# The order of small works at the pair boundaries of an attention kernel: three tables of unit numbers changed

## The reference

```python
x = x + _layernorm(_L0_attn_ref(_layernorm(x), wq, wk, wv, wo, q_norm_w, k_norm_w))
x = x + _layernorm(_L0_ffn_ref(_layernorm(x), gate_w, up_w, down_w, gate_s, up_s, down_s))
# attention: 32 query heads, 8 key/value heads of 64, RMS norm over the whole q and the whole k
xq = _rms_norm(x @ wq.T, q_norm_w, EPS)
xk = _rms_norm(x @ wk.T, k_norm_w, EPS)
xv = x @ wv.T
bias = where((dist <= 0) & (dist >= -256), slopes * dist, -inf)
attn = softmax(xq @ xk.T * scale + bias)
out = (attn @ xv) @ wo.T
# feed forward: ternary weights (-1, 0, 1) with a scale for each row
out = (silu((x @ gate_w.T) * gate_s) * ((x @ up_w.T) * up_s)) @ down_w.T * down_s
```

## Time and profile before

| | |
|---|---|
| median of 3 runs | 1192.66 us (1192.19 to 1193.7) |
| the profiled execution | 1192.59 us, span 1190.7 us |
| granted TensorE clock, mean | 0.998 |
| projection of four sequences | to about 291 us of the span |
| attention, pairs 0 to 3 (no output projection) | 291.1 to 414.6 us |
| attention, pairs 4 to 15 | 414.6 to about 882 us |
| rest | last output tiles, feed forward |

### The profile page before, as it was taken

The page is one execution under the profiler, slowest core; times in us unless marked ns, Lnnn a source line. Parts: engine busy times, 40 slices in busy tenths (PEclk is TensorE's granted clock), DMA queues, the critical chain, the costliest instruction groups (busy, mean ns, idle before and its releaser), DMA issues.

```text
span 1190.7 us, 26658 instructions
## 1 busy us (share of the span) xinstructions
PE 1161.0 (98%) x9016; PEld 991.1 (83%) x9016; DVE 888.5 (75%) x2329; ACT 743.6 (62%) x1583; POOL 304.6 (26%) x353
## 2 busy tenths in 40 slices
PE   7999999999999999999999999999999999999997
PEld 5878888887877798889988988898988888888876
DVE  5587778687899888888888888888866575645464
ACT  4645555455899888878888888888853443222230
POOL 3000000000788842423242333323211100202022
PEclk9999999999999999999999999999999999999999
DMA  5216355346676766556755575556445540303020
GB/s 177 106 45 247 143 201 223 124 195 255 209 237 232 246 208 201 170 190 197 220 159 187 182 226 163 154 171 209 138 134 186 168 141 2 107 1 107 1 71 37
DMA packets 100898, 189.55 MB, mean 159 GB/s; under 512 B 9376, under 2 KB 39072, under 8 KB 100768
## 3 DMA queue, kind: packets, MB, share of 16 engines
q1 hardware_dynamic: 100768, 187.88, 47.1%
HBM read 116.22 MB, written 71.63 MB: 158 GB/s over the span
## 4 chain that ended last, share of the span: by engine, by line
PE 92%; DVE 3%; ACT 2%; issue 1%; DMA 0%; POOL 0%; SPq 0%; POOLq 0%; DVEq 0%; ACTq 0%
PE bank L1408 21%; PE bank L1541 19%; PE bank L1473 15%; PE bank L1346 12%; PE bank L1434 12%; PE bank L1452 3%; PE bank L1450 3%; PE bank L1451 3%; PE bank L1462 2%; PE bank L1518 1%; PE bank L1373 1%; DVE pT_lo L1172 0%; ACT y_raw L937 0%; PE bank L1363 0%; ACT o_raw L925 0%
## 5 line engine op out<-in xcount | busy, mean ns | idle before, releaser
L802 ACT ACTIVATE p_sb<-u_sb,low 128x384 f32<-128x384 f32 (+2 forms) x512 | 271.7, 535 | 54.0 <-DVE low L1054 47.0
L1054 DVE CUSTOM_DVE_ANT_0 u_sb<-bank,bias 128x384 f32<-128x384 f32 (+2 forms) x512 | 229.1, 451 | 44.5 <-PE bank L1346 25.4
L1346 PE MATMUL bank<-k_st,q_st 128*128 128x384 f32 (+2 forms) x1024 | 252.3, 329 | 1.8 <-DVE low L1054 1.7
L1434 PE MATMUL bank<-ident,p_sb 128*128 128x128 f32 x1152 | 217.3, 279 | 11.6 <-DVE pT_lo L1172 3.6
L1168 DVE TENSOR_TENSOR pT_lo<-bank,pT_hi 128x384 f16<-128x384 f32 (+2 forms) x394 | 179.0, 454 | 32.1 <-ACT pT_hi L913 24.9
L1346 PEld LDWEIGHTS bank<-k_st,q_st 128*128 128x128 f32 x1024 | 169.0, 191 | 18.5 <-DVE low L1054 2.2
L913 ACT ACTIVATE pT_hi<-bank 128x384 f16<-128x384 f32 (+2 forms) x394 | 160.3, 407 | 37.5 <-PE bank L1434 35.4
L1434 PEld LDWEIGHTS bank<-ident,p_sb 128*128 128x128 f32 x1152 | 140.4, 140 | 42.2 <-ACT p_sb L802 18.3
L696 POOL TENSOR_TENSOR o_out<-o_raw,inv_sum 128x256 f32<-128x256 f32 x128 | 80.3, 628 | 319.4 <-DVE inv_sum L1180 319.4
L1541 PE MATMUL bank<-zT_hi,gu 128*128 128x512 f32 x352 | 139.2, 396 | 0.6 <-DVE hid L1297 0.6
L1541 PE MATMUL bank<-zT_lo,gu 128*128 128x512 f32 x352 | 138.1, 392 | 0.0
(11 more groups left out here) (134 smaller groups left out, 2309.0 us busy)
## 6 DMA issues: line engine op xcount, KB each, us to landing
q_st<-q_scr SPq DMA_DIRECT2D x32, 1024.0 KB, 8.0
q_scr<-qk SPq DMA_DIRECT2D x61, 512.0 KB, 2.7
k_st<-k_scr SPq DMA_DIRECT2D x64, 256.0 KB, 3.3
o_scr<-o_out SPq DMA_DIRECT2D x128, 128.0 KB, 3.5
o_in<-o_scr SPq DMA_DIRECT2D x16, 768.0 KB, 5.1
z_in<-z_scr SPq DMA_DIRECT2D x8, 1024.0 KB, 6.2
k_scr<-qk SPq DMA_DIRECT2D x12, 512.0 KB, 2.7
v_scr<-v_out SPq DMA_DIRECT2D x4, 1040.0 KB, 6.4
```

Source lines behind the costliest of these rows:

```text
L802: nc.scalar.activation(p_sb[:, u % RING, 0:w], u_sb[:, u % RING, 0:w], ACT.Exp, scale=-1.0, bias=low[:, u % RING:u % RING + 1]).then_inc(p ...
L1054: nc.vector.tensor_tensor_reduce(out=u_sb[:, u % RING, 0:w], in0=bank[u % 2][:, 0:w], in1=bias[2 * u // UNITS][:, u % REP, at:at + w], sca ...
L1346: mm = nc.tensor.matmul(bank[u % 2][:, 0:w], q_st[:, s, r, P * i:P * i + P], k_st[:, s, part, P * key:P * key + w], start=(part == 0), sto ...
L1434: mm = nc.tensor.transpose(bank[probability_bank(A)][:, P * j:P * j + P], p_sb[:, u % RING, P * j:P * j + P], ident[:])
```

## The change

Three tables and what hangs on them:

- `TAKE_Y_AT` 1 to 0 and `STATS_AT` 3 to 2: the copy of the accumulator and its statistics stand one unit earlier in pairs 5 to 15.
- Pair 0's four late norms move from units 2, 4, 18, 20 to 8, 12, 18, 22; the rounding and the split of norm f = 2 move from unit 0 to unit 5 (`LAST_EARLY_AT`); the split of the last value tile moves on VectorE from ahead of unit 0 to behind the bias of unit 2.
- `BITS_AT` (19, 20, 21) to (10, 19, 26), and SyncE issues the loads of a pair's bits near the end of the pair ahead of it, behind the last late store and ahead of the output tile `store_o(n, 1, 0)`.

```diff
-TAKE_Y_AT, STATS_AT, NORM_AT = 1, 3, 6
+TAKE_Y_AT, STATS_AT, NORM_AT = 0, 2, 6
...
-BITS_AT = (19, 20, 21)
+BITS_AT = (10, 19, 26)
...
+LAST_EARLY_AT = 5
 LATE_COUNTS = {0: 4, 1: 3, 2: 3, **{n: 1 for n in range(LAG, LAG + 7)}}
-LATE_AT = {4: (2, 4, 18, 20), 3: (4, 18, 20), 1: (17,)}
+LATE_AT = {4: (8, 12, 18, 22), 3: (4, 18, 20), 1: (17,)}
...
                     load_o(tile, last=True)
-                    if tile < IC:
-                        load_bits(tile)
                 store_late(n, 0, UNITS // 2)
...
                 store_late(n, UNITS // 2, UNITS)
+                if 0 <= tile + 1 < IC:
+                    load_bits(tile + 1)
                 if n == B * TT - 1:
                     load_o(tile + 2)
                 store_o(n, 1, 0)
...
-                    if n == 0 and u == 0:
+                    if n == 0 and u == LAST_EARLY_AT:
                         round_raw(B - 1, LATE - 1)
...
+            def split_v(b, n):
+
+                i = n - QC - KVC
+                dve.wait_ge(v_hi_ready, TT * b + i + 1)
+                nc.vector.tensor_tensor(v_out[:, :, i, 0:HD], bank[n % 4][:].rearrange("p (g d) -> p g d", g=G), v_out[:, :, i, HD:2 * HD],
+                                        ALU.subtract).then_inc(v_ready, 1)
...
+                        if n < NGEMM - 1 or not last:
+                            split_v(b, n)
...
-                    if n == 0 and u == 0:
+                    if n == 0 and u == AHEAD:
+                        split_v(B - 1, NGEMM - 1)
+                    if n == 0 and u == LAST_EARLY_AT:
                         split_raw(B - 1, LATE - 1)
```

## The result

The changed kernel takes 1196.8 us (median of 8 runs, 1195.89 to 1197.63) beside 1193.2 us of the kernel before (median of 8). The ratio is 1.0025, with a 95% interval of 1.0017 to 1.0034: 2.0 to 4.1 us slower. My forecast was 1189.5 us and its range ended at 1192.8.

The account below looks back on a forecast made before the run. Attention was taken as bounded by nearly full vector engines in full-width units, and by TensorE from pair 4 on. 1192.6 - 0.7 - 0.7 - 2.2 + 0.4 = 1189.4, said as 1189.5 us; range 1186.3 to 1192.8.

Parts of the forecast that it names:

- part 1: Start of pair 0, reordered value split, norm 2 and late norms: -1.75 us at unit 8, +1.05 for scalings, -0.7 us.
- part 3: Weight-bit gathers moved, 11 pairs: -2.2 us from units 20 and 21, +0.4 us at unit 10.
- Then split 0.6: Pair 0, unit 5: VectorE's split of norm 2 takes 0.6 us, after which biases 6 to 8 follow, bias 8 at 297.5.
- gap closed: Start of pair 0: the 1.67 us that unit 4's scores wait for VectorE's bias of unit 2 disappears.
- bias 2: Start of pair 0: the bias of unit 2 runs at 292.0 instead of 293.84, freeing unit 4's scores at 292.4.
- the wait of 1.10 us: Pair 0, unit 5: VectorE waits 1.1 us for ScalarE's rounding of norm 2, with bias 6 behind it.
- the clock falls later: Rival, chance 0.10: new gap ahead of unit 8 drops the clock in full-width units; saving less 1.65 us, 1191.1 us.
- The late norms: Pair 0: two scalings moved to units 8 and 12 cost +1.05 us; the fourth norm, unit 20 to 22, costs 0.
- Part 2: Accumulator's copy and statistics one unit earlier at 11 pair starts: net -0.06 us each, -0.7 us in all.
- Without the gather bias 21 starts when its scores end: Pair 13, units 20 to 24: bias 21 starts at 787.86, moving the chain by 0.18 to 0.20; -2.2 us over 11 pairs.
- The second term: Gathers now at units 10 and 26: unit 10's transposes may start 0.04 us late, +0.4 us over 11 pairs.
- the rival of uncovered gathers: Rival, chance 0.12: gathers in 384-wide units delay splits that reach TensorE; 6.6 us at half cover, 1195.6 us.

Follow-up runs that it names:

- the run of the start alone: Changed kernel with the accumulator's copy, statistics and weight bits put back, so only the first pair's start differs from the kernel before; 1196.0 us, 1.0020.
- the run with the bits alone: Kernel before with only the gathers moved to units 10, 19 and 26 and the bits' loads moved; 1194.7 us, 1.0009.

## Why the prediction was wrong

Two steps failed, and they cost about the same. The forecast had -0.7 us for part 1, and the runs found +2.8 (pair 0 +2.5, pair 1 +0.3); it had -1.8 us for part 3, and they found +1.4. None of my rivals had the mechanism of the first.

**The first step that failed** is the walk of part 1 at the words "Then split 0.6". I gave the split of norm 2 its duration from a row where GpSimd was idle, and placed it at unit 5, right where GpSimd begins the second bias behind bias 5. It took 2.38 us. All else of the walk up to there came about as written (gap closed, bias 2, the wait of 1.10 us). So bias 8 came not 1.75 us sooner but 0.19 later (8.36 against 8.17 us). With the collision taken away bias 8 stands at 6.66 us; the walk had 6.4 (its terms 295.7 + 0.6 + 1.0 give 297.3, and the 0.2 from there to its 297.5 it didn't name).

The Trainium skill (SBUF — State Buffer, "Who interferes with whom") states this rule: a VectorE instruction with two SBUF inputs contends with a GpSimd instruction that reads SBUF, and the second is blocked for the other's whole length. The traces agree that the second is held, and more often than where I met it: in the twelve kernels' profiles a VectorE instruction of 512 columns with two SBUF inputs is over 0.05 us longer than its kind 179 times, and each time it began under a GpSimd instruction over SBUF tiles of 256 columns or more and ends 0.54 to 0.55 us behind that one's end. I had not held my new order against it.

Ten of these cases are in the kernel before, so the price could have been read ahead of the forecast. The dearest stands in the projection, a sum of squares under GpSimd's first bias:

```profile
25.18 2.75 POOL L686 TENSOR_TENSOR bias<-dist,slopes 128x1536 f32<-128x1536 f32 x1 [4.84 <-PE bank L1408]
...
26.16 2.32 DVE L1138 TENSOR_TENSOR sum_sq<-sum_sq,square 128x512 f32<-128x512 f32 x1 [2.03 <-ACT square L884]
```

The same addition takes 0.69 us elsewhere; here it lasts 2.32 and ends 0.55 us behind GpSimd. In the changed kernel the split begins 0.92 us into a bias of 2.75, and 2.75 - 0.92 + 0.55 = 2.38, the measured length.

**The clock.** My rival "the clock falls later" came true on top. TensorE stood idle for 2.83 us, and soon after it the granted clock is 0.67 in units 8 to 11, which take 5.19 us; in the run with the scalings at 10 and 13, after a gap of 1.1 us, the same four units with one scaling as well take 3.83 us at a clock of 1.00. So the lower level, 1.2 GHz, cost about 1.36 us; the rival's 1.65 was its upper bound. (In the run of the start alone, where it fell sooner, the same sum over units 0 to 11 gives 0.9.) The slow stretch of the earlier trace rows is gone in return, but it lay in units where TensorE doesn't set the pace. The length of the gap alone doesn't decide: in the kernel before the clock fell behind a gap of 1.67 us, in the run with GpSimd's bias later it stayed at 1.00 behind gaps of 1.15 and 1.96 us. What does is not shown here.

**The late norms** were sized about right. Units 8 to 15 took 9.70 us instead of 7.39, +2.31; without the clock's 1.36 that is +0.95 against a forecast of +1.05, and units 16 to 31 take 15.48 us in both kernels. What I didn't see is pair 1, 0.28 us longer: GpSimd's cast of wo now lies over its scaling of unit 4, and the scaling takes 1.05 us in place of 0.77, with the same 0.55 us behind GpSimd's end. The two rows of the changed kernel:

```profile
330.58 0.61 POOL L709 CAST wo_hi<-wo_stage 128x512 fp32r<-128x512 f32 x1
...
330.69 1.05 DVE L1095 SCALAR_TENSOR_TENSOR raw_first<-raw_first,norm_w,inv_rms 128x512 f32<-128x512 f32 x1
```

**Part 2** was right in kind and a little small: -0.06 a pair said, -0.08 to -0.10 found. (The walk let the first product start 0.31 us sooner, where its row shows a wait of 0.26; nothing else hangs on that.)

**Part 3, the second step that failed,** was wrong in both terms. The first is the words "Without the gather bias 21 starts when its scores end". I started bias 21 at the modelled end of its scores, so it seemed 0.18 us late. But in the changed kernel, with no gather ahead, that bias starts at 792.55, 0.22 us behind the end of its scores (791.84 + 0.49), and in the kernel before it was the same 0.22: it starts at 788.04, and its scores end at 787.82 (787.34 + 0.48), not at my 787.86.

```profile
787.34 0.48 PE L1346 MATMUL bank<-k_st,q_st 128*128 128x256 f32 x2
```

From the modelled end of the scores to the bias it is 0.22 us in 71 of the 74 biases of the kernel before that wait for TensorE, so in this pair the gather was hidden already. In the mean of pairs 5 to 14 of the run with the bits alone, biases 21 and 22 do come sooner against bias 18, by 0.07 and 0.14 us, but by bias 23 only 0.05 of it is left. Found: about -0.05 us a pair in place of -0.20. The second term: the gather at unit 10 was to cost 0.04 and costs 0.13 (0.38 at first, of which TensorE's slack takes back 0.25); the one at unit 26 delays bias 27 by 0.5 us and costs nothing. Both stay under the 0.27 us at which I let the rival of uncovered gathers decide, so it was not this rival that came true. I also overlooked that the count in pair 15 moves with `BITS_AT[0]`: pair 15 is 0.54 us longer in the run with the bits alone.

The sum with what was found: pair 0 +2.5, pair 1 +0.3, part 2 -0.08 x 11 = -0.9, part 3 +0.08 x 11 + 0.5 = +1.4, together +3.3 us, beside a measured +3.6 (2.0 to 4.1). The lengths of the changed kernel's own pairs give +3.2.

What stays open: why a held instruction ends 0.55 us behind GpSimd's, less than its own 0.69 or 0.75 us. It could be that part of it had been done ahead, or that GpSimd's spans, which are rough, end early. An estimate speaks for the first: a bias takes 0.28, 0.42 and 0.56 us for 128, 256 and 384 columns, so 0.14 for 128 columns more and 0.56 for 512, with another 0.14 that doesn't grow; a held instruction would have that fixed part behind it and only its columns ahead. No run tells the two apart.

## What to carry to other kernels

When an instruction moves, its duration must be read beside what the other engines do at the new place, not only its waits: list GpSimd's instructions there first, and for each moved VectorE instruction ask what it reads. With two inputs in SBUF it was held every time that it began under GpSimd work over wide tiles, a copy and a `tensor_scalar` over one SBUF tile were held too, and a bias or split with one input in PSUM never was. If GpSimd is under way already, the length is what is left of GpSimd's instruction plus 0.55 us for 512 columns, and such cases can be looked up in the trace of the kernel before. An instruction counts as late only against the handoff that its kind always shows (0.22 us here from the modelled end of the scores to the bias), not against the modelled end. And where a table's number is read in more than one place, each reader moves with it.

## What the runs showed of the hardware

The hold works in both directions. With the gather of unit 10 running from 779.79 us, GpSimd's normalisation of the output, ready behind VectorE's reciprocal, has its start in the record only half a microsecond in (with GpSimd free and no gather running it starts 0.20 us behind the reciprocal), and it ends 0.47 us behind the gather:

```profile
779.64 0.18 DVE L1186 RECIPROCAL inv_sum<-o_raw 128x4 f32<-128x4 f32 x1
...
780.30 0.65 POOL L697 TENSOR_TENSOR o_out<-o_raw,inv_sum 128x256 f32<-128x256 f32 x1 [1.84 <-DVE inv_sum L1186]
```

In other places it is recorded as running 0.85 to 0.97 us in place of 0.61 under a gather, twenty times between 449 and 838 us, and each of these ends 0.47 or 0.48 us behind the gather. They are nearly all of GpSimd's 6.2 us more of busy time. What they cost wasn't measured apart; only SyncE's stores wait for this output.

Not every GpSimd instruction over SBUF holds VectorE. Its inverse root of four columns lasts 1.52 us, and in the kernel before a scaling and a split run beside it at their usual length:

```profile
125.47 1.52 POOL L657 TENSOR_TENSOR rstd<-var_eps,minus_half 128x4 f32<-128x4 f32 x1 [68.64 <-DVE var_eps L1023]
...
126.03 0.74 DVE L1094 SCALAR_TENSOR_TENSOR raw_last<-raw_last,norm_w,inv_rms 128x512 f32<-128x512 f32 x1
...
126.69 0.68 DVE L1090 TENSOR_TENSOR qk<-raw_last,qk 128x512 fp32r<-128x512 f32 x1
```

It is the same in every profile, twice. That a hold lasts as long as GpSimd reads, and not as long as its instruction, would fit; no run tests it. So the rule, as cited above, is wider than what these traces show.
